# Five message-passing layers on one core: per-tile copies beside the chased scatters, early node loads of the first layer, four late fetch rounds

## The reference

```python
h = relu(layernorm(x));  x += relu(segment_sum((h[src] @ W[edge_type]), dst) + h @ W_loop + b)        # REL
h = relu(layernorm(x));  x += attention over edges: q from dst, k and v from src, summed over rows=src # ATT
h = relu(layernorm(x))                                                                                 # SAGE0, SAGE1
g = relu(layernorm(h @ Ws0.T + segment_mean(h[src], dst) @ Wn0.T + b0))
x += layernorm(g @ Ws1.T + segment_mean(g[src], dst) @ Wn1.T + b1)
h = relu(layernorm(x));  x += segment_sum over edges and self loops of (h @ W) * norm                 # GCN
```

## Time and profile before

| | |
|---|---|
| median, lowest, highest of three runs | 3697.28, 3694.93, 3700.2 us |
| profiled execution: time, span | 3701.02 us, 3699.3 us |
| busy in the span | PE 2617.9, DVE 2511.4, ACT 1948.6, POOL 2612.2 us |
| DMA | 638.73 MB, mean 173 GB/s |
| chain that ended last | issue 6%; POOL 5%; PE 5%; ACT 4%; DMA 3%; DVE 2% |

### The profile page before, as it was taken

The page is one execution under the profiler, slowest core; times in us unless marked ns, Lnnn a source line. Parts: engine busy times, 40 slices in busy tenths (PEclk is TensorE's granted clock), DMA queues, the critical chain, the costliest instruction groups (busy, mean ns, idle before and its releaser), DMA issues. The chain is left out here.

```text
span 3699.3 us, 82926 instructions
## 1 busy us (share of the span) xinstructions
PE 2617.9 (71%) x19724; PEld 2288.0 (62%) x19724; DVE 2511.4 (68%) x11513; ACT 1948.6 (53%) x5393; POOL 2612.2 (71%) x2673
## 2 busy tenths in 40 slices
PE   3899998888466666630018887767888775887888
PEld 3899997666465555530007765546776665776777
DVE  5677776889555445538864448883448887665998
ACT  1333334777454444421117777763446664776777
POOL 3677773666788888855457778767778784777876
PEclk9999999999787777765559999998999998999999
DMA  7544444888433333339972239982229997222998
GB/s 277 215 149 140 147 147 136 268 267 269 125 42 41 41 41 41 41 50 317 311 229 53 52 109 297 294 287 67 52 60 332 335 337 246 53 52 79 309 311 287
DMA packets 336597, 638.73 MB, mean 173 GB/s; under 512 B 62000, under 2 KB 90832, under 8 KB 335208
## 3 DMA queue, kind: packets, MB, share of 16 engines
q1 hardware_dynamic: 241758, 502.00, 41.0%
q0 software_dynamic: 90944, 133.85, 16.3%
q10 hardware_dynamic: 3786, 1.65, 0.2%
HBM read 371.35 MB, written 277.50 MB: 175 GB/s over the span
## 5 line engine op out<-in xcount | busy, mean ns | idle before, releaser
L750 POOL DMA_INDIRECT got<-rows,gidx x588 | 606.3, 1031 | 225.8 <-issue 173.3
L797 POOL DMA_INDIRECT sums<-got,sidx x588 | 614.9, 1046 | 168.7 <-issue 156.5
L1056 ACT ACTIVATE n_h<-ring 128x128 f32<-128x128 f32 x1176 | 482.7, 482 | 56.5 <-DVE ring L1730 45.8
L971 ACT ACTIVATE psum_out<-bank 128x132 f32<-128x132 f32 x784 | 218.8, 279 | 531.4 <-PE bank L1223 530.7
L1324 PE MATMUL bank<-ring,ident 128*128 128x128 f32 x2352 | 459.3, 277 | 0.0
L1204 PE MATMUL bank<-parked 128*128 128x128 f32 x3136 | 388.7, 278 | 11.9 <-DVE parked L1558 11.9
L1189 PE MATMUL bank<-ident,e_h 128*128 128x128 f32 x588 | 96.0, 287 | 408.0 <-ACT e_h L934 408.0
L1204 PEld LDWEIGHTS bank<-parked 128*128 128x128 f32 x3136 | 371.5, 194 | 13.7 <-issue 8.6
L811 POOL DMA_INDIRECT attsums<-ring,sidx x196 | 312.3, 1594 | 80.2 <-issue 64.5
L1324 PEld LDWEIGHTS bank<-ring,ident 128*128 128x128 f32 x2352 | 361.6, 194 | 0.0
L1461 DVE COPY gidx<-src_i 128x4 int32 (+1 forms) x227 | 45.2, 199 | 465.2 <-DMA got<-rows,gidx 204.4
(11 more groups left out here) (183 smaller groups left out, 7250.7 us busy)
## 6 DMA issues: line engine op xcount, KB each, us to landing
ring<-sums SPq DMA_DIRECT2D x392, 264.0 KB
ring<-rows SPq DMA_DIRECT2D x392, 264.0 KB, 4.7
rows<-ring SPq DMA_DIRECT2D x294, 264.0 KB
attsums<-parked SPq DMA_DIRECT2D x49, 528.0 KB
rows<-parked SPq DMA_DIRECT2D x49, 528.0 KB
ring<-attsums SPq DMA_DIRECT2D x98, 264.0 KB
rowsg<-ring SPq DMA_DIRECT2D x98, 264.0 KB
ring<-rowsg SPq DMA_DIRECT2D x98, 264.0 KB
```

The costliest lines, as they stand in the source:

```text
L750: pool.indirect_dma_start(out=got[:, b, j, 0:width], out_offset=None, in_=table[:, :], in_offset=bass.IndirectOffsetOnAxis(ap=gidx[:, b, j ...
L797: pool.indirect_dma_start(out=sums[:, :], out_offset=bass.IndirectOffsetOnAxis(ap=sidx[:, b, j:j + 1], axis=0), in_=got[:, b, j, :], in_of ...
L1056: last = nc.scalar.activation(n_h[:, b, k, :], x_data(phase, g)[:, k, :], ACT.Relu, bias=x_col(phase, g, k, COL_C), scale=x_col(phase, g, ...
```

## The change

1. REL's sums are loaded by the same due counts as the other phases' (`load_s`, `rel_landed`, a fourth row in `due_i`), and the wait for all scatters before the node loads is gone, so that SyncE may load x and sums of the first groups while REL's edges still run.
2. The zeroing of `attsums` and `rows1` is done in 24 steps of twice the size.
3. The last four rounds (`LATE`) of destination rows are no longer fetched behind REL's nodes, but in the first turns of ATT, straight to `parked`.
4. In the chase, each scatter of round r - 1 is followed by the copy of one tile of round r, with one semaphore count for each tile.
5. `rowsg`, the table between SAGE0 and SAGE1, has rows of 128 instead of 132 values; its tiles are dense on chip.

```diff
...
+    LATE = 4
...
-    rowsg = nc.dram_tensor("rowsg", (N, W), fp32, kind="Internal").ap()
+    rowsg = nc.dram_tensor("rowsg", (N, D), fp32, kind="Internal").ap()
...
+        s_padded = sem("s_padded")
...
+        late_fetched = [Signal(sem(f"late_fetched{r}"), 16 * TPR) for r in range(LATE)]
...
-        lent = Signal(sem("lent"), 1)
+        lent = Signal(sem("lent"), TPR)
...
-            return dense(g.mod(8)) if phase == REL else x_rows(phase, g)[:, :, 0:D]
+            return dense(g.mod(X_SLOTS.get(phase, 8))) if phase in (REL, SAGE1) else x_rows(phase, g)[:, :, 0:D]
...
-            return dense(RING - 4 + g.mod(4)) if phase == GCN else out_rows(phase, g)[:, :, 0:D]
+            return dense(RING - 4 + g.mod(4)) if phase in (SAGE0, GCN) else out_rows(phase, g)[:, :, 0:D]
...
-        ZEROED_TABLES = 2 * (ROUNDS + 1)
-        ZROUND = (PAD + 1) // (ROUNDS * P)
-        assert 0 < PAD + 1 - ROUNDS * ZROUND * P <= P
+        ZSTEPS = ROUNDS // 2
+        ZROUND = (PAD + 1) // (ZSTEPS * P)
+        ZTAIL = PAD + 1 - ZSTEPS * ZROUND * P
+        ZEROED_TABLES = 2 * (ZSTEPS + 2)
...
-            run_steps(sp, [(zero_tables, 0)], ROUNDS, 1)
+            run_steps(sp, [(zero_tables, 0)], ZSTEPS, 1)
             for table in (attsums, rows1):
-                sp.dma_start(table[ROUNDS * ZROUND * P:PAD + 1, :], zeros[0:PAD + 1 - ROUNDS * ZROUND * P, 0:W])\
+                sp.dma_start(table[ZSTEPS * ZROUND * P:PAD + 1 - ZTAIL % P, :].rearrange("(p r) c -> p (r c)", p=P),
+                             zeros[:, 0:ZTAIL // P * W]).then_inc(s_zero_tables, 16)
+                sp.dma_start(table[PAD + 1 - ZTAIL % P:PAD + 1, :], zeros[0:ZTAIL % P, 0:W])\
                     .then_inc(s_zero_tables, 16)
...
                 elif phase == REL:
                     sp.wait_ge(s_zero_sums, 16 * ZERO_COUNT)
                     sp.wait_ge(s_zero_tables, 16 * ZEROED_TABLES)
-                    for b in range(2):
-                        sp.wait_ge(scattered[b].sem, parity_first(1, b) * 16 * TPR)
-                elif phase == SAGE0:
                     sp.wait_ge(s_due, 1)
...
-                    if phase in CHASED:
+                    if phase in SEG_PHASES:
 
                         gate(sp)
-                        base = rounds_landed.credit + parked_before(phase)
-                        due = sp.value_load(due_i[0:1, CHASED.index(phase), at(g)], min_val=base, max_val=base + ROUNDS)
+                        base = rounds_landed.credit + seg_index(phase) * ROUNDS
+                        due = sp.value_load(due_i[0:1, seg_index(phase), at(g)], min_val=base, max_val=base + ROUNDS)
...
-                def copy_parked(r):
-                    b = r.mod(GOT)
+                def rel_landed(r):
+                    b = r.mod(2)
+                    pool.wait_ge(scattered[b].sem, scattered[b].after(r.div(2), parity_first(seg_index(phase), b)))
+                    pool.sem_inc(rounds_landed.sem, 1)
+
+                def landed_before(r):
                     if r.i is not None or r.offset >= 3:
                         round_landed(r.back(3))
-                    nc.gpsimd.tensor_copy(sidx[:, b, :], last_i[:, bass.ds(r.scaled(TPR), TPR)])
-                    pool.wait_ge(parked_ready.sem, parked_ready.after(r, parked_before(phase)))
...
+                def copy_parked(r, j):
+                    b = r.mod(GOT)
+                    if j == 0:
+                        nc.gpsimd.tensor_copy(sidx[:, b, :], last_i[:, bass.ds(r.scaled(TPR), TPR)])
+                        pool.wait_ge(parked_ready.sem, parked_ready.after(r, parked_before(phase)))
+                        gate(pool)
+                    nc.gpsimd.tensor_copy(got[:, b, j, :], spans[:, bass.ds(r.scaled(TPR * W, j * W), W)])\
+                        .then_inc(lent.sem, 1)
+
+                def scatter_copied(r, j):
+                    b = r.mod(GOT)
+                    if j == 0 and r.i is None and r.offset == ROUNDS - 1:
+                        round_landed(r.back(2))
+                    pool.wait_ge(lent.sem, lent.after(r, parked_before(phase), j + 1))
                     gate(pool)
-                    nc.gpsimd.tensor_copy(got[:, b, :, :], parked[:, bass.ds(r.scaled(TPR), TPR), :])\
-                        .then_inc(lent.sem, 1)
-
-                def scatter_copied(r):
-                    b = r.mod(GOT)
-                    if r.i is None and r.offset == ROUNDS - 1:
-                        round_landed(r.back(2))
-                    pool.wait_ge(lent.sem, lent.after(r, parked_before(phase)))
-                    gate(pool)
-                    for j in range(TPR):
-                        pool.indirect_dma_start(
-                            out=sums[:, :], out_offset=bass.IndirectOffsetOnAxis(ap=sidx[:, b, j:j + 1], axis=0),
-                            in_=got[:, b, j, :], in_offset=None,
-                            bounds_check=bound, oob_is_err=False).then_inc(scattered[r.mod(2)].sem, 16)
+                    pool.indirect_dma_start(
+                        out=sums[:, :], out_offset=bass.IndirectOffsetOnAxis(ap=sidx[:, b, j:j + 1], axis=0),
+                        in_=got[:, b, j, :], in_offset=None,
+                        bounds_check=bound, oob_is_err=False).then_inc(scattered[r.mod(2)].sem, 16)
...
+                def late_dst(r):
+                    if r.i is None and r.offset < LATE:
+                        f = ROUNDS - LATE + r.offset
+                        for j in range(TPR):
+                            t = f * TPR + j
+                            pool.indirect_dma_start(
+                                out=parked[:, t, :], out_offset=None, in_=rows1[:, :],
+                                in_offset=bass.IndirectOffsetOnAxis(ap=dst_i[:, t:t + 1], axis=0),
+                                bounds_check=bound, oob_is_err=False).then_inc(late_fetched[r.offset].sem, 16)
+                    if r.i is None and 2 <= r.offset < LATE + 2:
+                        pool.wait_ge(late_fetched[r.offset - 2].sem, 16 * TPR)
+                        pool.sem_inc(dst_parked.sem, 1)
...
-                                     (lambda r: gather(r, range(2, 4)), 0), (lambda r: add_pair(r, 1), 4)],
+                                     (lambda r: gather(r, range(2, 4)), 0), (late_dst, 0), (lambda r: add_pair(r, 1), 4)],
...
-                    run_steps(pool, [(gather, 0), (scatter, 3 + extra(phase))], ROUNDS, 2, behind=1)
+                    run_steps(pool, [(gather, 0), (scatter, 3 + extra(phase)), (rel_landed, 5 + extra(phase))], ROUNDS, 2, behind=1)
...
-                    run_steps(pool, [(copy_parked, 0), (scatter_copied, 1)], ROUNDS, GOT, behind=2)
+                    turn = [(landed_before, 0)]
+                    for j in range(TPR):
+                        turn += [(lambda r, j=j: scatter_copied(r, j), 1), (lambda r, j=j: copy_parked(r, j), 0)]
+                    run_steps(pool, turn, ROUNDS, GOT, behind=2)
...
-                    run_steps(pool, [(fetch_dst, 0), (park_dst, 1)], ROUNDS, 2, behind=2)
+                    nc.gpsimd.memset(parked[:, TILES - 1, :], 0.0).then_inc(s_padded, 1)
+                    pool.wait_ge(s_padded, 1)
+                    run_steps(pool, [(fetch_dst, 0), (park_dst, 1)], ROUNDS - LATE, 2, behind=2)
...
-                        rows = x_rows(phase, g)[:, k, 0:D] if phase == SAGE1 else n_h[:, b, k, :]
+                        rows = x_data(phase, g)[:, k, :] if phase == SAGE1 else n_h[:, b, k, :]
...
-            for n, phase in enumerate(CHASED):
+            for n, phase in enumerate(SEG_PHASES):
                 last = nc.vector.tensor_scalar(due_f[:, n:n + 1], due_rounds[:, :],
-                                               float(rounds_landed.credit + parked_before(phase)), None, ALU.add)
+                                               float(rounds_landed.credit + seg_index(phase) * ROUNDS), None, ALU.add)
             last.then_inc(s_due_f, 1)
...
-                    nc.vector.tensor_tensor(rows[:, :, 0:D], n_t[:, g.mod(DEEP), :, :],
+                    nc.vector.tensor_tensor(rows, n_t[:, g.mod(DEEP), :, :],
```

More of the change, by code:

```diff
@@ L228, in gnn_stack_kernel @@
         due_rounds = sb("due_rounds", [P, 1])
-        due_f = sb("due_f", [P, len(CHASED)])
-        due_i = sb("due_i", [1, len(CHASED), P], i32)
+        due_f = sb("due_f", [P, len(SEG_PHASES)])
+        due_i = sb("due_i", [1, len(SEG_PHASES), P], i32)
         zero_at = early(1)
@@ L546, in gnn_stack_kernel @@
         ZERO_COUNT = ZPARTS + (1 if ZLEFT_A else 0) + (1 if ZLEFT - ZLEFT_A else 0)
-        ZEROED_TABLES = 2 * (ROUNDS + 1)
-        ZROUND = (PAD + 1) // (ROUNDS * P)
-        assert 0 < PAD + 1 - ROUNDS * ZROUND * P <= P
+        ZSTEPS = ROUNDS // 2
+        ZROUND = (PAD + 1) // (ZSTEPS * P)
+        ZTAIL = PAD + 1 - ZSTEPS * ZROUND * P
+        ZEROED_TABLES = 2 * (ZSTEPS + 2)
+        assert ZTAIL // P and ZTAIL % P
         @block.sync
@@ L630, in load_x @@
                     table = node_in[phase]
```

(12 more changed lines are left out.)

## The result

The changed kernel takes 3777.58 us (median of 4 runs, 3772.01 to 3785.13), the kernel before in the same comparison 3698.74: a ratio of 1.0208, 95% interval 1.0174 to 1.0241. It is slower by 79 us, where 47 had been forecast. The profiled execution took 3774.32 us with a span of 3772.6, against a span of 3699.3 before; these two traces differ by 73.3 us.

| stage | before, us | after, us | difference | forecast |
|---|---|---|---|---|
| start to the last scatter of REL's edges | 611.0 | 636.7 | +25.7 | +14 |
| REL's nodes, ATT, to SAGE0's first gather | 1310.2 | 1319.2 | +8.9 | +22 |
| SAGE0: first scatter of the chase to SAGE1's first gather | 319.9 | 328.9 | +9.0 | +9 |
| SAGE1: first scatter to GCN's first gather | 364.6 | 386.8 | +22.2 | -2 |
| GCN: first scatter to the end | 305.3 | 313.7 | +8.4 | +4 |

A forecast was written before the change was run, and what follows sets the result against it. Four paces were named: GpSimd in ATT's edges, DMA in SAGE1's nodes, GpSimd's chase in SAGE0, a store-and-load loop in REL's nodes. Terms +27 - 7 + 2 + 13 - 2 + 14 = +47 us gave 3744 (median), range 3686 to 3780.

The forecast's parts named there:

- Count read: REL's nodes: reading the due count delays each load and store by 1.16 us, 0.30 us a group, +27 us.
- First loads early: Start of REL's nodes: VectorE's 6.79 us wait for the first x goes, -7 us, paid out once.
- Late rounds: Into ATT: gathers start 19 us earlier, but 16 fetches come back in ATT at +21 us; net +2.
- Scatter and copy in turn: Chase: 0.19 us more a round, full in SAGE0, half in GCN, none in SAGE1; +13 us.
- not in SAGE1, whose nodes follow the DMA: SAGE1's chase: the longer round counted at nothing, as the DMA engines were taken to pace the nodes.
- Narrow `rowsg`: SAGE1's nodes: one of four transfers per group gets 8 KB smaller, 0.7% of 358 us, -2 us.
- Double zero steps: REL's edges: zeroing in 24 double steps makes gathers land late, +14 us, bounds 0 and +44.
- The pile: REL's edges: seven piled-up zero steps take 47 us instead of 23, two more late rounds, +8 us.
- steady term of 0.35 us: REL's edges: 17 more rounds with a double pair of zero steps cost 0.35 us each, +6 us.
- the zeroing is free: Rival for REL's edges: the double zero steps cost nothing; chance 0.13, with the count covered too 0.10.
- covered read: Rival for REL's nodes: SyncE's idle time covers the count's read, +20 us in all, 3717; chance 0.13.
- The chase faster: Rival for the chase: copies vanish under the scatters, which get short, -47 instead of +13, 3684; chance 0.17.

The follow-up runs named there:

- the last experiment: Changed kernel with 49 zero steps, count read first, chase scattering straight from parked sums, a tiny fill behind each scatter: 3679.80 us, 0.9950 of the kernel before (3700 chip).

## Why the prediction was right, and where its terms were off

The sign, the mechanism of most parts and the range (3686 to 3780) held, the last barely. The sizes were off by 32 us in all, and that the range held is in part luck: the count's read was put 9 us too high, and the alternation and the double zero steps 40 us too low. The parts as measured are 18 for the read, -7 for the first loads, nothing for the late rounds and the narrow `rowsg`, 43 for the alternation and 24 for the zero steps: 78 us, where 74 to 79 were measured for the whole.

- **Count read, forecast +27.** The mechanism was right: the read alone spreads the products. 97 turns of 3.628 - 3.447 us are 17.6 us, and reading it before the wait gave 16.3 of them back. The term took the delay of a load from GCN, 1.16 us; here it was 0.88 - 0.16 = 0.72, a third of which is 0.24 us a turn, where 0.18 was measured. The read ahead of the wait was timed only together with other parts put back, and on the 4560 chip it gave back half.
- **First loads early, -7.** VectorE's 6.79 us of idle time are gone: it starts at 633.67, as the edges end, and its first add comes 9.1 us after REL's last scatter instead of 16.1.
- **Late rounds, +2.** 21 us off the way into ATT and 21 us more in ATT's edges. From VectorE's last add of a product to ATT's last add, the kernel before took 694.1 us, the changed one 693.4 and the last experiment 694.7.
- **Scatter and copy in turn, +13.** The part alone costs 43 us. GCN (4 forecast, 8 measured) is the sum of rows that it was said to be, 0.20 us a round where 0.19 was worked out, and should have been counted in full; SAGE0 (9 forecast) took 9 in the first pair of traces, 14 for the part alone and 17 in the changed kernel on that chip. The step that failed is "not in SAGE1, whose nodes follow the DMA". It is true of the kernel before, but only by some 9 us. In every kernel that GpSimd paces, the stage ends 31 to 33 us after SAGE1's last scatter (382.9 - 351.5, 384.1 - 351.4, 391.6 - 358.2); before, the chase was 320.9 us, so it would have allowed 353 where the nodes took 361.5. With a chase of 281.7 us in the last run the stage still takes 365.9, its DMA share 1.00: that is the nodes' own pace, and SyncE's waits for the chase, 0.7 us in 150 before and 10.1 with the alternation, say the same. The alternation made the chase 30.6 us longer, which goes past this margin: 351.5 + 32 - 361.5 = 22, and 21 were measured (the 32 is read from the same kernels, so this shows that the account is consistent, and no more). The forecast put 9 us on a chase and never set the two paces of SAGE1 beside each other; and its copy of 0.32 us, right in SAGE0 and GCN (0.32 and 0.30 with the alternation alone), takes 0.41 to 0.43 there. Its pauses were read in SAGE0 too.
- **Narrow `rowsg`, -2.** Nothing: SAGE1 takes 384.1 us with it and 382.9 without.
- **Double zero steps, +14.** 24 to 26 us. The pile came as forecast, with two more late rounds. The steady term of 0.35 us was too low: gathers land 1.3 us later (3.0 us after their issue instead of 1.7), four times the margin of 0.33 us. From 200 to 330 us a zero packet of 8448 B takes 0.34 us at the median in the changed kernel, and one of 4224 B 0.17 in the kernel before; the 1.3 us are more than one such packet takes. That the zeroing is free, to which the forecast gave 0.13 alone and 0.10 together with a covered read, is refuted on this kind of chip. Packet size and bytes per round were doubled together, and no run tells why it is 1.3 us.
- **The chase faster, 0.17** (room between the scatters makes them short, faster) is refuted on the 3700 chips: SAGE1's scatters take 1.159 us with a copy behind each (alternation alone, 2850 to 3000 us) and took 1.144 before. A rival that no row could show is what the 4560 chips do.

That the change was slower holds for one kind of chip. On the other the kernels that keep the alternation took 0.967 to 0.970 of the time of the kernel before. The changed kernel as it stands was not timed there.

## What to carry to other kernels

Where two engines pace a stage nearly alike, write down both paces, and the margin between them, before calling an edit to one of them free: GpSimd's chase had 9 us of cover in SAGE1 and got 31 more. Price an instruction in the stage where it will run: the same copy took 0.30 us in one layer and 0.43 in another. Put a slow read (0.64 us here) ahead of the wait that it need not follow, and where the landing of gathers leaves a small margin (0.33 us here), keep the writes that go beside them in small steps, spread over all the rounds: with double steps the gathers landed 1.3 us later, and the edges were 24 to 26 us longer on a 3700 chip. And time a change of 2% on more than one chip.

## What had not been expected of the hardware

- Two kinds of chips, by 23%, for one program. On the longer kind, signals between other engines arrive microseconds late while GpSimd issues indirect DMAs back to back (median 16 to 19 us in SAGE0's chase without a break, 0.8 to 2.6 with breaks); the alternation gained some 175 us there and lost 43 on the other kind. Whether the break itself or its length matters was not tested there. The gathers of SAGE0 are longer there too, 338 to 351 us against 255. Why the kinds differ, no run shows.
- A one-column fill of 0.12 us between two scatters is next to free: it starts as the scatter ends, and the pause behind it is 0.19 instead of 0.30 us.
- Every second scatter can take 1.30 us instead of 0.97, as the rows of SAGE0 in the last run show; in GCN they don't. The load of the DMA engines alone does not explain it: their share is 0.96 in SAGE0 (2200 to 2450 us, 1.12 us a scatter on the mean) and 0.98 in GCN (3420 to 3600 us), where a scatter takes 0.97.
